# A transformer block on one core: key blocks regrouped so that one transfer serves a quadrant, moves by SyncE alone, a table of PSUM banks

## What is computed

```
h = layernorm(x, ln1);  x = attention(h, h,   sa_w*) + x     # 16 heads of 64
h = layernorm(x, ln2);  x = attention(h, ctx, ca_w*) + x
h = layernorm(x, ln3);  a, gate = split(h @ ff_w1 + b1)
x = (a * gelu(gate)) @ ff_w2 + b2 + x
# attention: softmax(q k^T / 8) v, then @ wo + bo
```

## Time and profile before

| | |
|---|---|
| median of 3 runs | 2963.45 us |
| profiled execution, its own time | 2961.8 us |
| its span, first to last instruction | 2959.7 us |
| instructions | 76813 |
| TensorE weight loads, busy | 2509.0 us, 85% |
| VectorE busy | 2300.7 us, 78% |
| ScalarE busy | 1915.2 us, 65% |
| GpSimd busy | 1437.6 us, 49% |
| moved by DMA | 413.02 MB, mean 140 GB/s |
| self-attention, change of pass, cross-attention, feed-forward | to about 1200, 1340, 2420 and 2960 us |

### The profile page before, as it was taken

The page is one execution under the profiler, slowest core; times in us unless marked ns, Lnnn a source line. Parts: engine busy times, 40 slices in busy tenths (PEclk is TensorE's granted clock), DMA queues, the critical chain, the costliest instruction groups (busy, mean ns, idle before and its releaser), DMA issues.

```text
span 2959.7 us, 76813 instructions
## 1 busy us (share of the span) xinstructions
PE 2883.2 (97%) x25236; PEld 2509.0 (85%) x25236; DVE 2300.7 (78%) x3513; ACT 1915.2 (65%) x6041; POOL 1437.6 (49%) x1290
## 2 busy tenths in 40 slices
PE   7999999999999999899999999999999989999999
PEld 6788888888888888777888888888888879999999
DVE  7788888888888888887888888888888865555554
ACT  6566677667666666666777777777777654444443
POOL 3444444444444444454555555555555445545454
PEclk9999999999999999999999999999999999999999
DMA  5655555555555555565666655665666542222222
GB/s 138 183 148 148 148 148 147 147 147 147 148 147 147 148 147 144 144 164 158 159 163 159 161 159 159 159 162 159 160 161 161 154 127 79 73 86 71 82 78 61
DMA packets 533674, 413.02 MB, mean 140 GB/s; under 512 B 170864, under 2 KB 520432, under 8 KB 533360
## 3 DMA queue, kind: packets, MB, share of 16 engines
q1 hardware_dynamic: 451792, 336.71, 41.9%
q10 hardware_dynamic: 81824, 75.56, 10.0%
HBM read 94.52 MB, written 49.02 MB: 48 GB/s over the span
## 4 chain that ended last, share of the span: by engine, by line
PE 63%; SPq 15%; ACT 7%; DVE 6%; issue 4%; DMA 3%; ACTq 2%; POOL 0%; DVEq 0%
PE unit_ps L562 33%; SPq L492 14%; PE s_ps L562 12%; PE o_ps L587 10%; PE s_ps L575 8%; ACT probs L793 5%; DVE neg_max L975 3%; DMA rows_in<-rows_t_dram 2%; DVE blocks L989 2%; ACTq L809 2%; ACT v_f L837 1%; ACT qk_hi L831 1%; DVE hT_lo L1017 1%; ACT x_n L773 0%; DVE hT_lo L1013 0%
## 5 line engine op out<-in xcount | busy, mean ns | idle before, releaser
L1196 POOL TENSOR_TENSOR probs<-probs,row_inv 128x1024 f32<-128x1024 f32 x512 | 968.7, 1897 | 1009.8 <-DVE row_inv L980 1009.8
L793 ACT ACTIVATE probs<-s_ps,neg_max 128x256 f32<-128x256 f32 x2048 | 952.0, 491 | 270.0 <-DVE neg_max L975 269.7
L975 DVE TENSOR_REDUCE neg_max<-s_ps 128x4 f32<-128x1024 f32 x512 | 616.2, 1204 | 101.0 <-PE s_ps L575 98.5
L989 DVE STREAM_TRANSPOSE blocks<-probs 128x1024 f32<-128x1024 f32 x512 | 632.7, 1236 | 20.0 <-POOL probs L1196 17.4
L562 PE MATMUL unit_ps<-hT_hi,w_hi 128*128 128x256 f32 x2048 | 585.7, 288 | 37.3 <-ACT v_f L837 32.1
L562 PE MATMUL unit_ps<-hT_hi,w_lo 128*128 128x256 f32 x2048 | 556.7, 278 | 0.0
L587 PE MATMUL o_ps<-pT,v_f 128*64 128x256 f32 x4096 | 502.0, 387 | 15.1 <-DMA pT<-blocks 9.4
L562 PE MATMUL unit_ps<-hT_lo,w_hi 128*128 128x256 f32 x1792 | 498.6, 278 | 0.0
L1000 DVE TENSOR_TENSOR qk_lo<-unit_ps,qk_hi 128x512 fp32r<-128x512 f32 x512 | 354.2, 692 | 180.4 <-ACT qk_hi L831 171.5
L793 ACT ACTIVATION_READ_ACCUMULATOR probs<-s_ps,neg_max 128x1 f32 x2048 | 451.4, 220 | 0.0
L562 PEld LDWEIGHTS unit_ps<-hT_hi,w_hi 128*128 128x128 f32 x2048 | 386.4, 189 | 73.3 <-ACT v_f L837 46.9
(11 more groups left out here) (68 smaller groups left out, 5957.5 us busy)
## 6 DMA issues: line engine op xcount, KB each, us to landing
pT<-blocks SPq DMA_DIRECT2D x3200, 64.0 KB, 2.0
pT<-blocks ACTq DMA_DIRECT2D x896, 64.0 KB, 2.1
rows_t_dram<-row_blocks SPq DMA_DIRECT2D x91, 256.0 KB, 2.4
rows_in<-rows_t_dram SPq DMA_DIRECT2D x91, 256.0 KB, 2.9
x_res<-in_x_dram SPq DMA_DIRECT2D x32, 256.0 KB, 2.8
x_sa_dram<-x_out SPq DMA_DIRECT2D x32, 256.0 KB, 2.2
x_ln<-x_sa_dram ACTq DMA_DIRECT2D x32, 256.0 KB, 3.1
ctx_in<-in_ctx_dram SPq DMA_DIRECT2D x32, 256.0 KB, 2.9
```

What stands on the lines that cost most here:

```text
L793: op = nc.scalar.activation(probs[:, m % 2, r, :], s_ps[:, m % 2, r // IT, r % IT * S:(r % IT + 1) * S], ACT.Exp, bias=neg_max[:, m % RING ...
L975: nc.vector.tensor_reduce(neg_max[:, m % RING, :], s_ps[:, m % 2, :, :].rearrange("p h (i j) -> p (h i) j", j=S), AX_X, ALU.max, negate=Tr ...
L989: nc.vector.transpose(blocks[:, n % 2, m % 2, :, :].rearrange("p b (j r c) -> p r j b c", j=IT, c=BLK), probs[:, m % 2, :, :].rearrange("p ...
L1196: nc.gpsimd.tensor_tensor(probs[:, m % 2, :, :], probs[:, m % 2, :, :], row_inv[:, m % RING, :].unsqueeze(2).broadcast_to([P, ROWS, S]), A ...
```

## The change

Keys are taken into blocks by every fourth one: block b holds the keys 4c+b. After a 32x32 transpose, row c of block b is key 4c+b, so the four blocks of a source quadrant, 32 partitions with four rows each, go to all 128 partitions in order by one transfer of 256 KB. `blocks` and `pT` get the quadrant ahead of the head pair. The transpose now reads the probabilities with a step of four floats and writes runs of 32 as before. SyncE issues all four moves of a step; ScalarE issues none. The rows' transposes do the same: `move_rows` replaces store and load, in the place of the store (step 3, for batch t+2), with four moves of 64 KB inside SBUF; the permuted write of x_n and the host's reordering of weights go. Banks come from a table.

```diff
-MOVES = 16 * NB * NB
+MOVES = 16 * NB
+BANK_OF = {("v", 0, 0): 0, ("qk", 2): 2, ("qk", 3): 1, ("v", 0, 1): 0,
+           ("qk", 4): 2, ("qk", 5): 1, ("wo", 0): 0,
+           ("v", 1, 0): 2, ("x",): 0, ("qk", 6): 1, ("qk", 7): 0, ("v", 1, 1): 2,
+           ("qk", 0): 1, ("qk", 1): 0, ("wo", 1): 2}
 def bank_of(unit):
-    return [u for u, _ in ORDER].index(unit) % BANKS
+    return BANK_OF[unit]
...
-        blocks = sb("blocks", [P, 2, 2, NB, IT * ROWS * BLK])
-        pT = sb("pT", [P, 2, 2, NB, IT * ROWS * BLK])
+        blocks = sb("blocks", [P, 2, NB, 2, IT * ROWS * BLK])
+        pT = sb("pT", [P, 2, NB, 2, IT * ROWS * BLK])
-        row_blocks = sb("row_blocks", [P, DK * NB, IT * BLK])
-        rows_in = sb("rows_in", [P, DK, S])
+        row_blocks = sb("row_blocks", [P, NB, DK, IT * BLK])
+        rows_in = sb("rows_in", [P, NB, DK, IT * BLK])
...
-            def store_row_blocks(sems, b, whole):
...
-            def load_rows_transposed(sems, b, whole):
...
+            def move_rows(sems, b, whole):
+                ready, shifted = in_register(b - whole + 1), in_register(b)
+                sp.wait_ge(sems.row_blocks, ready)
                 sp.wait_ge(sems.h_done, shifted)
+                for i in range(NB):
+                    sp.dma_start(rows_in[:, i, :, :], row_blocks[i * BLK:(i + 1) * BLK, :, :, :]).then_inc(sems.rows_ld, 16)
...
                 for i in range(NB):
-                    for j in range(NB - 1 if i < pass_of(b, home).by_act else NB):
-                        sp.dma_start(pT[j * BLK:(j + 1) * BLK, n % 2, :, i, :],
-                                     blocks[i * BLK:(i + 1) * BLK, n % 2, :, j, :]).then_inc(landed(b, n, home)[0], 16)
+                    sp.dma_start(pT[:, n % 2, i, :, :],
+                                 blocks[i * BLK:(i + 1) * BLK, n % 2, :, :, :]).then_inc(landed(b, n, home)[0], 16)
...
-                if blocks_next(t, parts):
-                    load_rows_transposed(at, t + 1, WHOLE)
...
                     if n == 3 and blocks_ahead(t, parts):
-                        store_row_blocks(at, t + 2, WHOLE)
+                        move_rows(at, t + 2, WHOLE)
...
-            def move_blocks(b, n, home):
...
-                    act.dma_start(pT[j * BLK:(j + 1) * BLK, n % 2, :, i, :],
-                                  blocks[i * BLK:(i + 1) * BLK, n % 2, :, j, :]).then_inc(landed(b, n, home)[0], 16)
...
-                nc.vector.transpose(row_blocks[:].rearrange("p e (i r) -> p i e r", i=IT),
-                                    x_n[:].rearrange("p i (e c) -> p i e c", c=BLK)).then_inc(sems.row_blocks, 1)
+                nc.vector.transpose(row_blocks[:].rearrange("p j k (i r) -> p i k j r", i=IT),
+                                    x_n[:].rearrange("p i (k c j) -> p i k j c", k=DK, c=BLK)).then_inc(sems.row_blocks, 1)
...
-                nc.vector.transpose(blocks[:, n % 2, m % 2, :, :].rearrange("p b (j r c) -> p r j b c", j=IT, c=BLK),
-                                    probs[:, m % 2, :, :].rearrange("p r (j b c) -> p r j b c", j=IT, c=BLK)
+                nc.vector.transpose(blocks[:, n % 2, :, m % 2, :].rearrange("p b (j r c) -> p r j b c", j=IT, c=BLK),
+                                    probs[:, m % 2, :, :].rearrange("p r (j c b) -> p r j b c", j=IT, c=BLK)
                                     ).then_inc(at.blocks_done, 1)
```

More of the change, by code:

```diff
@@ L64, in user_before @@
     place = [u for u, _ in ORDER].index(unit)
-    if not isinstance(t, int):
-        place -= BANKS
-        while ORDER[place] == (("x",), "nxt"):
-            place -= BANKS
-        u, part = ORDER[place]
-        return u, batch_of(t - 1 if place < 0 else t, part)
-    while t >= -1:
-        place -= BANKS
+    while not isinstance(t, int) or t >= -1:
+        place -= 1
         if place < 0:
@@ L75, in user_before @@
         u, part = ORDER[place]
-        if t >= -1 and 0 <= batch_of(t, part) < batches and (u != ("x",) or by_tensor(batch_of(t, part))):
-            return u, batch_of(t, part)
+        if bank_of(u) != bank_of(unit):
+            continue
+        b = batch_of(t, part)
+        if not isinstance(t, int):
+            if u != ("x",):
+                return u, b
+        elif t >= -1 and 0 <= b < batches and (u != ("x",) or by_tensor(b)):
+            return u, b
     return None
@@ L258, in block_kernel, with __init__ @@
         class Pass:
-            def __init__(self, name, norm, x_in, x_to, has_ctx, weights, first, by_act):
-                self.by_act = by_act
+            def __init__(self, name, norm, x_in, x_to, has_ctx, weights, first):
                 self.norm, self.x_in, self.x_to, self.has_ctx, self.first = norm, x_in, x_to, has_ctx, first
@@ L772, in normalise @@
                 for it in range(IT):
-                    op = nc.scalar.activation(shuffled(x_n[:, it, :]) if whole else x_n[:, it, :],
-                                              straight(x_ln[:, it, :]) if whole else x_ln[:, it, :], ACT.Identity,
-                                              bias=ln_shift[:, it:it + 1], scale=rstd[:, it:it + 1])
+                    op = nc.scalar.activation(x_n[:, it, :], x_ln[:, it, :], ACT.Identity, bias=ln_shift[:, it:it + 1],
+                                              scale=rstd[:, it:it + 1])
                 op.then_inc(sems.ln_done, 1)
@@ L954, in normalise @@
             def normalise(ph, b):
-                whole = isinstance(b, int) and b < FF_WHOLE
                 dve.wait_ge(ph.stats_done, b + 1)
```

51 lines of the change are left out of this document (12 added, 39 removed).

## The result

The changed kernel takes 3144.2 us, the median of four runs (3143.7 to 3145.3), beside 2962.9 for the kernel before: a ratio of 1.0615, with a 95% interval of 1.0597 to 1.0634. The forecast was 2936, faster. What came is the first rival, "strided reads cost", which gave 3141.

The account below looks back on a forecast made before the run. TensorE's instruction order was taken as the bound. Terms -10 - 3 - 9 - 5 = -27 gave 2961.8 - 27 + 1.65 = 2936 us, likeliest 2915 to 2948, full range 2910 to 3160.

Parts of the forecast that it names:

- strided reads cost: Rival: VectorE's strided transpose reads slow every attention step, +0.78 us a transpose, 3141 us in all; chance 0.38.
- Bound: Whole kernel: TensorE's instruction order bounds it, at most 76.5 us of waits to gain; VectorE next, 82% and 87% busy.
- VectorE's reads, 0: VectorE's transposes of probabilities and rows: reading every fourth word costs nothing; upper end +1.4 us a transpose.
- The rival's price: VectorE's transposes: 0.77 ns an element, taken from permuted writes, so +0.78 us a transpose, +6.3 a batch.
- its own threshold of 0.35: Attention: the strided-read rival decides from about +0.35 us a transpose, +2.8 a batch, what idle VectorE can give up.
- The rival's conversion: Attention batches: VectorE's added time makes them 39.5 to 40 us, +2.2 x 31 and +3.9 x 32 = +193.
- third to half: Attention batches: this share of VectorE's idle 6.8 and 4.6 us, mostly waiting for ScalarE, stays under the strided-read rival.
- Issuing, 0 in steady steps and -5: Merged moves on SyncE: no gain in steady steps; -5 us in first batches, change of pass and end.
- rows, -9: Rows by four quadrant moves without the round trip: half of 19.2 us of TensorE's waits on value copies, -9.
- Banks, -10 and -3: Bank table: self-attention step 2 from 9.58 to 9.21 us, -10 over 28 steady batches; cross-attention -3, another wait replacing it.
- Feed-forward, 0: Feed-forward part: the four moves ahead of the output's store cost nothing, since TensorE is never idle there.
- none but the self-attention gain: Upper end of the sum's own range: only the self-attention gain comes, given as 2952 us.

Follow-up runs that it names:

- experiment 1: The changed kernel with only the probability transposes reading runs of 32 adjacent floats again, softmax weights meeting other keys' values: 2938.5 us.
- experiment 2: The kernel before with only the probability transposes reading every fourth float, softmax weights meeting other keys' values: 3156.8 us.
- Experiment 6: The changed kernel with adjacent reads in the probability transposes and the old banks in turn, without the table: 2952.3 us.
- experiment 11: The kernel before with the bank table, and TensorE's wait on the context's remainder moved between qk 0's Q and K halves: steady cross-attention batch 35.82 against 35.84 us.

## Why the prediction was wrong, by its own steps

*Bound.* TensorE's order was the bound, and VectorE was next with 82 and 87%. Right, and it was the warning: VectorE had 6.8 and 4.6 us a batch to give, and the change took 6.4 + 0.4.

*VectorE's reads, 0: the step that failed.* "I take 0: the row that is nearest in engine, operation and direction is the transpose itself, which only changes its read's step." That row is an adjacent read; it shows nothing of what changes. The only rows that varied the stride were writes, and they pointed the right way. Beside the rest of the change the term is +206 us (after against experiment 1), alone +195 (experiment 2), not 0. The rule of the Trainium skill quoted there, "Vector Engine (DVE) Microarchitecture Reference", section "Measured stream behaviour on trn2", came out on the right side: its 1.73 against 1.05 ns is +0.68 a column.

*The rival's price.* +0.78 us a transpose, from 0.77 ns an element, where the read cost 0.79. That closeness is luck. The 0.77 is the mean of two records, 715 and 487 ns, against 405. In the kernel after the same two instructions write in order, and so do the first six of ScalarE's x_n. VectorE's two after; then ScalarE's six, before and after:

```profile
L933 DVE TENSOR_SCALAR x_n<-x_ln,mean_var,rstd x2: 401/503/605, 2581.5 to 2582.0; 128x256 f32<-128x256 f32 x2
```

```profile
L773 ACT ACTIVATE x_n<-x_ln,ln_shift,rstd x6: 805/881/927, 8.4 to 57.9; 128x256 f32<-128x256 f32 x6
```

```profile
L760 ACT ACTIVATE x_n<-x_ln,ln_shift,rstd x6: 587/612/630, 7.9 to 60.7; 128x256 f32<-128x256 f32 x6
```

The first of VectorE's two takes 605 ns in order as well; in both kernels it runs beside GpSimd for 0.46 us. So the permuted write cost VectorE 110 and 86 ns, 0.43 and 0.34 an element, half of what was taken from it. At that price the rival would have been +0.4 us a transpose, barely past its own threshold of 0.35. ScalarE's write cost about 1.05 ns an element.

*The rival's conversion.* Its +2.2 and +3.9 a batch are +2.0 and +3.7 in steady batches; less what the irregular ones gain, as it foresaw. It had nothing for the feed-forward part, where +19 us came, so part of the closeness of 3141 to 3144 is two errors that cancel. VectorE kept 7% of its time idle, 2.9 us a batch: of the 6.8 us in self-attention that is within the "third to half" that was assumed, of the 4.6 in cross-attention it is more.

*Issuing, 0 in steady steps and -5; rows, -9.* Experiment 6 bears out the zero: steady batches as before. Sizes were off: an issue takes 0.68 us (median), not 0.5, and four in a row some 3.8 us; the landing takes 4.6 us, not at most 3.1. Four such moves still fit into 13.6 us: from the first issue to the last landing of a step it is 7.3 us, 9.0 at most. Of the irregular batches -14 was asked: experiment 6 has -8 up to the first store (97.2 against 105.3), and -0.31 x 31 - 0.33 x 31 = -20 in the two passes, of which next to nothing is in steady batches. The place was right and the size half of it.

*Banks, -10 and -3.* Experiment 1 against 6: -0.37 in each steady batch of self-attention, 12.8 us of the span in all. Step 2 takes 9.21 us, as said (score products at 948.02 and 957.23). With the table alone it still takes 9.54 in the batch shown (939.06 to 948.60), since a move came last: the term needs the other part of the change. In cross-attention the wait on the context's remainder took the place, as written, and experiment 11 showed more behind it.

*Feed-forward, 0.* Wrong, +0.63 a batch, by the strided row transpose and the four moves. "TensorE is never idle there" gave no price, because an idle share of zero says nothing of how close the next engine's chain is.

*The sum without the read.* Experiment 1 is that: -21.5 us by the spans, in which the feed-forward part has +18. Without that part it is -40 where -27 was asked, the difference being the irregular batches. (The sum's own upper case, "none but the self-attention gain", is 2953 by its terms, not 2952.)

## What to carry to other kernels

A change that moves a stride from one place to another has its price there, whatever the element count: look for any row of the trace that changes the step, on a write if need be, and multiply by the elements before calling it free. See first what ran beside that row: here half of the price that was read came from somewhere else. Then set the product against the idle time of that engine in the same stretch; once it is used up, the loss shows in every batch. And a stall removed by one part of a change can be refilled by what another part would have removed, so gains are to be tried together as well as alone.

## What the runs showed of the hardware

Of VectorE's 32-blockwise transpose of 128x1024 fp32: reads at steps of 4 and 8 bytes both take 1.235 us, 16 bytes 2.04, 32 bytes 2.15. The edge lies between 8 and 16 bytes, not at adjacency. Writes of 256 floats at a step of 16 bytes cost VectorE 0.34 and 0.43 ns an element more than writes in order, and ScalarE about 1.05.

Of VectorE beside GpSimd: the context's remainder (128x256, SBUF to SBUF) takes 0.95 to 0.97 us in every record that GpSimd's own half of it overlaps, and 0.40 to 0.46 in every other, in all fourteen kernels here; the scaling of rows likewise takes 0.83 or 0.40 in the kernel after. The transposes (701 to 711 ns for rows before) and the remainders from PSUM (0.69 us) show no such step.

Of TensorE at a clock of 1.00: a moving operand of 256 fp32r columns starts every 0.117 us if read in order, and every 0.23 at a step of 16 bytes, at a step of 8, and in pairs 16 bytes apart. The step that is free for VectorE halves TensorE's rate.

Of the DMA: 256 KB from 32 partitions of SBUF to 128 land in 4.6 us (3.6 to 6.7), where 64 KB took 2.0; the loads of the same stretches slowed as well, x_ln from memory on ScalarE's queue from 3.1 to 4.9 us, while in the feed-forward part, where there are no such moves, they take 2.7 us, beside 2.8 before.
